# A new order of attention's instruction queues, and eight units in place of four in a turn of its loop

## The chip, the cores and the metric

One core of one Trainium2 chip runs the whole program. The time is that of one execution on the device in microseconds (us); of several runs of one kernel the median counts. The engines are TensorE (PE, with its weight loads as PEld), VectorE (DVE), ScalarE (ACT), GpSimd (POOL) and SyncE (SP, which here only issues DMAs). Each works through its own list of instructions strictly in order, and they meet only at semaphores.

## What is computed

A decoder layer on x of 4 x 512 x 512 in float32: attention of the delta-rule kind with two decay rates, then a state-space mixer with a second input, then a feed-forward block with eight low-rank experts; after each, a layer norm over the sum with the residual. The part that the change touches is attention:

```python
def step(S, inp):                                  # for each head and batch, over 512 tokens
    qt, kt, vt, bt, gt = inp
    Sd = S * gt[..., None]
    v_pred = jnp.einsum('bhk,bhkv->bhv', kt, Sd)
    S_new = Sd + jnp.einsum('bhk,bhv->bhkv', kt * bt[..., None], vt - v_pred)
    ot = jnp.einsum('bhk,bhkv->bhv', qt, S_new)
    return (S_new, ot)
...
q = short_conv(x @ wq, conv_q_w).reshape(B, T, H, DK)      # k and v likewise, H = 16, DK = DV = 128
# beta, decay and lam come from a small MLP on |v|, |v - k @ proxy_w|, their cosine and an entropy
o_fast = delta_rule(qs, k_unit, v, beta_fast, decay_fast)
o_slow = delta_rule(qs, k_unit, v, beta_slow, decay_slow)
o = lam[..., None] * o_fast + (1.0 - lam[..., None]) * o_slow
g = (x @ g1_w @ g2_w + g2_b).reshape(B, T, H, DV)
o = o / rms * onorm_w * jax.nn.sigmoid(g)
return o.reshape(B, T, H * DV) @ wo
```

## The kernel before

`attn_stage` handles 64 units, one for each head and batch, batches innermost. The 512 tokens of a unit are four chunks of 128. Each unit passes through a pipeline that is six units deep, so that in one slot the engines work on several units at once: the projections and convolutions of the unit three (K, V) or two (Q) ahead, its norms and the small MLP, the decay products and the inverse of the triangular matrices of the unit itself, the recurrence over the four chunks of the unit before it, and the output gate and the store of older ones.

There is no scheduler. In each engine's block a function `slot(s)` writes out by hand the order of that engine's steps, `s` being the unit; `late = s.at(-1)` names the same step for the slot before, which lets a step that belongs to unit n stand at the start of the next slot. `over_units` calls the slot for units -3 to 5 in straight code, then for four units in each turn of a hardware loop (13 turns, 52 units), then for the rest in straight code. In the loop the values that a wait looks for are worked out from the turn (`due`, `head_due`, `head`).

The steps that the prediction speaks of, by the functions they are in:

- PE: `products(level)`, seven levels (L525 for levels 0 to 4, L531 for 5, L535 for 6); each multiplies slices of `ks` and `nq`. `w_fine_sum` (L549) and `x_fine_sum` (L560), steps of the inverse. `recur_even` (L573 turns `ks`, L578 multiplies `nq` with the state), `recur_u` (L593), `recur_odd` (L605, L609, L616): the recurrence. `project` (L503): one of four steps of a 128x512 projection of K, V or Q. Small steps: `turn_feats` (L713), `hidden_1` (L718), `hidden_2` (L722), `heads_out` (L726), `turn_v` (L666), `proxy_v` (L672), `gate_logits` (L706), `turn_rows` (L697), `mean_square` (L692); `w_64_sum` (L650) and `y_64_sum` (L658).
- DVE: `decay_nq(level)` (L1175 twice, then L1183), which waits for `products(level)` and which `products(level + 1)` waits for; `seed_y` (L1221), `keep` (L1194), `turn_x0` (L1227), `grow` (L1203, L1207); `convolve` (L1151, three instructions); `new_state` (L1234, L1238), `residual` (L1254); `prepare_nq` (L1306, L1310), once for -k and once for the query, after which `products(0)` of the next unit may run; `set_diag` (L1214), which waits until POOL's `spread_apt` (L1459) has read `apt_fine` of the unit before.
- ACT: copies from PSUM, `tap` (L846), `silu` (L858), `exp_e1` (L1018), `exp_tot` (L1023), `root_rows` (L1029), `log_mean` (L995), `log_err` (L991), `hide_1` (L906), `copy_feats` (L1038), `copy_w` (L867, L870, L873). When a function is of another table set than the last, an ACT_TABLE_LOAD stands ahead of it.
- SP: the rows that carry gates and decays go to DRAM and come back broadcast to all partitions, four waits and loads one after another.

## Time and profile before

| | us |
|---|---|
| median of 3 runs | 4910.75 |
| lowest and highest | 4907.41, 4925.25 |
| profiled execution | 4893.68 |
| its span, first to last instruction | 4891.9 |
| attention, first to last `mean_square` | 264 to 3326 of the span |
| PE busy in the span | 4244.3 (87%) |
| DVE, ACT, POOL busy in the span | 3329.3, 2248.5, 834.9 |

The rest of the span is the state-space mixer (to about 4119) and the feed-forward block, which the change leaves alone. "Idle before" at a group or a row is how long its engine did nothing before it, with who ended that; "issue" means that it waited for no event that the profile shows. L692 runs once for each unit, so the starts of its rows mark the units. PEclk is the granted clock as a share of the full 2.4 GHz; 0.5 is 1.2 GHz.

### The profile page before, as it was taken

The page shows a single profiled execution, that of the slowest core. Times are in us where ns is not written, and L with a number is a line of the kernel's source. Part 1 is how long each engine was busy: PE and PEld are TensorE (multiplying, and loading weights), DVE is VectorE, ACT ScalarE, POOL GpSimd, SP SyncE. Part 2 cuts the span into 40 slices and gives each one's busy share as a digit, 9 for nine tenths or more (in the row PEclk, how much of TensorE's full clock was granted, in tenths as well). Part 3 has the DMA queues.
Part 4 walks back from the last instruction along what each step waited for, and adds up shares of the span by engine and source line. Part 5 has one row for each costly group of instructions (what it writes and reads, how often), then busy time and mean ns, then how long its engine had stood idle before and what let it go on. Part 6 is the DMA issues. An engine that isn't in the chain of part 4 may idle for free. (4 is left out here: it accounts for less than half of the span.)

```text
span 4891.9 us, 184831 instructions
## 1 busy us (share of the span) xinstructions
PE 4244.3 (87%) x76786; PEld 2657.1 (54%) x76786; DVE 3329.3 (68%) x5635; ACT 2248.5 (46%) x5484; POOL 834.9 (17%) x1800
## 2 busy tenths in 40 slices
PE   6789898988989888898988899975887786999999
PEld 4566666665666656666666666662333333444444
DVE  2678787777778777787777777864999995122121
ACT  2455565655556555555555555644344432111111
POOL 0222222322222222222222232220000000000000
PEclk9899999999999999999999999987898997999999
DMA  1111211112121111211111111112232334000000
GB/s 50 61 52 57 62 49 54 62 45 68 43 65 52 52 60 43 66 52 53 58 53 59 58 53 56 62 45 104 78 95 82 91 95 160 1 26 9 18 18 9
DMA packets 131630, 278.08 MB, mean 57 GB/s; under 512 B 20668, under 2 KB 62032, under 8 KB 127200
## 3 DMA queue, kind: packets, MB, share of 16 engines
q1 hardware_dynamic: 126176, 258.29, 16.8%
q8 instruction: 641, 10.50, 0.9%
q10 hardware_dynamic: 4608, 7.60, 0.4%
q14 instruction: 205, 1.68, 0.1%
HBM read 235.17 MB, written 30.67 MB: 54 GB/s over the span
## 5 line engine op out<-in xcount | busy, mean ns | idle before, releaser
L503 PE MATMUL a_pb<-a_x_t,a_w_qkv 128*128 128x512 f32 x1536 | 825.0, 634 | 24.4 <-DMA a_w_qkv<-in_w_qkv 12.2
L1175 DVE TENSOR_TENSOR a_nq<-a_nq,a_tot 128x512 f32<-128x512 f32 x768 | 516.8, 714 | 157.4 <-PE a_pb L535 62.1
L1151 DVE SCALAR_TENSOR_TENSOR a_acc<-a_pb,a_taps,a_acc 128x511 f32<-128x511 f32 (+2 forms) x576 | 429.7, 746 | 67.0 <-ACT a_acc L846 35.3
L1773 PE MATMUL m_p_y<-m_h,m_ident 128*128 128x512 f32 x512 | 292.2, 686 | 143.3 <-DVE m_h L1973 143.3
L525 PE MATMUL a_pb<-a_nq,a_ks 128*32 128x32 f32 x20480 | 250.6, 201 | 145.1 <-DVE a_ks L1183 126.6
L503 PEld LDWEIGHTS a_pb<-a_x_t,a_w_qkv 128*128 128x128 f32 x1536 | 250.4, 195 | 131.2 <-issue 104.6
L525 PEld LDWEIGHTS a_pb<-a_nq,a_ks 128*32 128x32 f32 x20480 | 218.6, 112 | 188.4 <-DVE a_nq L1175 135.2
L2241 PE MATMUL f_pb<-f_x_t,f_w_gu 128*128 128x512 f32 x704 | 308.0, 592 | 0.0
L549 PE MATMUL a_pb<-a_x_fine,a_apt_fine 32*32 32x16 f32 x16384 | 203.7, 183 | 107.3 <-issue 106.0
L1967 DVE TENSOR_TENSOR_SCAN m_h<-m_da,m_h 128x2048 f32<-128x2048 f32 x64 | 283.1, 4424 | 5.9
L549 PEld LDWEIGHTS a_pb<-a_x_fine,a_apt_fine 32*32 32x32 f32 x16384 | 173.5, 108 | 203.5 <-issue 189.8
L560 PEld LDWEIGHTS a_pb<-a_w_fine,a_y_fine 32*32 32x32 f32 x16384 | 176.9, 109 | 189.5 <-issue 178.9
L1183 DVE TENSOR_TENSOR a_ks<-a_ks,a_tot 128x512 f32<-128x512 f32 x384 | 274.5, 715 | 0.0
L2295 ACT ACTIVATE f_gate<-f_pb 128x512 f32<-128x512 f32 x132 | 78.8, 597 | 411.7 <-PE f_pb L2241 275.4
L1773 PEld LDWEIGHTS m_p_y<-m_h,m_ident 128*128 128x128 f32 x512 | 107.5, 220 | 293.4 <-DVE m_h L1973 170.2
L560 PE MATMUL a_pb<-a_w_fine,a_y_fine 32*32 32x16 f32 x16384 | 207.7, 183 | 66.1 <-issue 61.4
L1737 PE MATMUL m_p_o<-m_w_o,m_o_t 128*128 128x512 f32 x512 | 256.9, 622 | 0.0
L1194 DVE COPY_PREDICATED a_apt_fine<-a_mask_u,a_pb 128x256 f32<-128x256 int32 x320 | 179.4, 561 | 106.5 <-PE a_pb L549 106.4
L1896 ACT ACTIVATE m_da<-m_delta,m_neg_a 128x511 f32<-128x511 f32 x256 | 166.7, 711 | 182.5 <-DVE m_h L1967 180.1
L885 ACT COPY a_u_sb<-a_pb 128x256 f32<-128x256 f32 x256 | 95.4, 373 | 296.0 <-PE a_pb L593 296.0
L2241 PEld LDWEIGHTS f_pb<-f_x_t,f_w_gu 128*128 128x128 f32 x704 | 133.4, 190 | 166.4 <-issue 166.4
L2373 DVE TENSOR_TENSOR f_h_base<-f_gate,f_pb 128x512 f32<-128x512 f32 x44 | 30.2, 686 | 277.6 <-ACT f_gate L2295 277.6
(278 smaller groups left out, 8927.3 us busy)
## 6 DMA issues: line engine op xcount, KB each, us to landing
a_rows<-rows SPq DMA_DIRECT2D x192, 512.0 KB, 3.9
a_amp_sums<-amp_sums SPq DMA_DIRECT2D x64, 508.0 KB, 3.6
attn_o<-a_o_t SPq DMA_DIRECT2D x64, 256.0 KB, 2.6
m_b_rows<-ssm_bc SPq DMA_DIRECT2D x64, 256.0 KB, 3.7
m_c_rows<-ssm_bc SPq DMA_DIRECT2D x64, 256.0 KB, 4.6
m_o_t<-attn_o SPq DMA_DIRECT2D x14, 1024.0 KB, 8.6
a_w_qkv<-in_w_qkv SPq DMA_DIRECT2D x51, 256.0 KB, 2.8
f_w_gu<-in_w_gu SPq DMA_DIRECT2D x3, 1536.0 KB, 17.3
```

The lines of the kernel that those rows point to most:

```text
L503: mm = nc.tensor.matmul(pb[:, V_BANK if i == P_V else KQ_BANK], w_qkv[:, i, k], x_t[:, k, b * T:(b + 1) * T], start=(k == 0), stop=(k == D ...
L525: mm = nc.tensor.matmul(out.rearrange("p k (s h) -> p k s h", h=hs), ks[:, n2, rate, at], right(nq[:, n2, rate, :, at], hs), start=True, s ...
L549: mm = nc.tensor.matmul(w_psum[q, i].rearrange("p (s h) -> p s h", h=hs), apt_fine[q, i, NEG_K], left(x_fine[q, i:i + 1], hs)[:, 0], start ...
L560: mm = nc.tensor.matmul(x_psum[q, i], y_fine[q, i], w_fine[q, i], start=True, stop=True, tile_position=(g * BW, g * BW))
L1151: last = nc.vector.scalar_tensor_tensor(acc[:, i, d:T], src[:, 0:T - d], taps[:, i, 3 - d:4 - d], acc[:, i, d:T], ALU.mult, ALU.add)
L1175: last = nc.vector.tensor_tensor(part, part, spread(blocks, shape), ALU.mult)
L1183: nc.vector.tensor_tensor(part, part, spread(blocks.rearrange("p (s two) -> p s two", two=2)[:, :, 1:2], [P, T // hs, hs]), ALU.mult).then ...
L1194: nc.vector.copy_predicated(right(apt_fine[:].rearrange("p i k t -> p (i k) t"), hs), spread(compact(mask_u[:, level:level + 1], hs), [P, ...
L1737: mm = nc.tensor.matmul(p_o[:], o_t[:, q % 2, head], w_o[:, head], start=(head == 0), stop=(head == H - 1), skip_group_check=True)
L1773: nc.tensor.matmul(p_y[:, et], ident[:], h[:, (b * DS + n) % 3, et], start=(n == 0), stop=(n == DS - 1), skip_group_check=True).then_inc(s ...
L1967: nc.vector.tensor_tensor_scan(steps, da[:, row % 2].rearrange("p e t -> p (e t)"), steps, 0.0, ALU.mult, ALU.add).then_inc(scanned, 1)
L2241: mm = nc.tensor.matmul(out, w_gu[:, side, k, cols], x2_t[:, b % 2, k], start=(k == 0), stop=(k == DC - 1), skip_group_check=True)
```

## The change

Three things. The loop's turn has eight units (`PER_TURN = 2 * B`), so 52 units are six turns, and four more units stand in straight code behind it; `due`, `head_due`, `head` and `stored_due` follow. The steps of PE, ACT, DVE and POOL stand in another order. And the waits are fitted to that order: `keep(1)` waits for `products(1)`, the column `decay` is loaded ahead of `exp_tot`, which now comes first, and POOL drains at the start of two steps.

```diff
-FIRST_TURN, TURNS = 6, (UNITS - 12) // B
+FIRST_TURN, PER_TURN = 6, 2 * B
+TURNS = (UNITS - 12) // PER_TURN
...
     with engine.Fori(0, TURNS) as turn:
-        for j in range(B):
+        for j in range(PER_TURN):
             slot(Slot(FIRST_TURN + j, turn))
-    for n in range(FIRST_TURN + B * TURNS, UNITS + 4):
+    for n in range(FIRST_TURN + PER_TURN * TURNS, UNITS + 4):
         slot(Slot(n))
...
                 def exp_e1(s):
-                    if s.batch(1) == 0:
-                        head_col(decay, s, 1, C_DECAY)
...
                 def exp_tot(s):
+                    if s.batch(1) == 0:
+                        head_col(decay, s, 1, C_DECAY)
...
                     if level == 0:
                         need(dve, w_sum, s.due(-1, 6, 4))
-                    elif level > 1:
+                    elif level == 1:
+                        dve.wait_ge(product, s.due(0, LEVELS, 2))
+                    else:
                         dve.wait_ge(w_sum, s.due(0, 6, level - 1))
...
                 def gates_vals(s):
+                    pool.drain()
...
                 def norms_dens(s):
+                    pool.drain()
...
                 def slot(s):
-                    soon = s.at(1)
-                    if s.has(2):
-                        make_feats(s)
-                    if s.has(0):
-                        spread_y(s)
...
+                    late = s.at(-1)
+                    if late.has(1):
+                        gates_vals(late)
+                    if late.has(0):
+                        spread_apt(late)
+                    if late.has(2):
+                        norms_dens(late)
```

On PE, from `products(0)` to `products(1)`, both on the same line: before,

```order
L525 MATMUL a_pb<-a_nq,a_ks 32x32 x32
L569 REGISTER_ALU
L573 MATMUL a_pb<-a_sum_w,a_ks 128x128 x2
L503 MATMUL a_pb<-a_x_t,a_w_qkv 128x512
L593 MATMUL a_pb<-a_r_sb,a_y_inv 128x128 x2
L722 MATMUL a_pb<-a_hid,a_w_diag 128x128
L514 REGISTER_ALU
L525 MATMUL a_pb<-a_nq,a_ks 32x32 x32
```

and after:

```order
L526 MATMUL a_pb<-a_nq,a_ks 32x32 x32
L651 MATMUL a_pb<-a_x_half,a_apt 64x64 x8
L504 MATMUL a_pb<-a_x_t,a_w_qkv 128x512
L570 REGISTER_ALU
L574 MATMUL a_pb<-a_sum_w,a_ks 128x128 x2
L714 MATMUL a_pb<-a_sum_w,a_feats 16x128
L656 REGISTER_ALU
L659 MATMUL a_pb<-a_y_inv,a_w 64x64 x8
L515 REGISTER_ALU
L526 MATMUL a_pb<-a_nq,a_ks 32x32 x32
```

`w_64_sum`, `turn_feats` and `y_64_sum` have come in between; `recur_u(0)` and `hidden_2` now stand between `products(1)` and `products(2)`, with `hidden_1`, `w_fine_sum(1)` and `recur_odd(0)`.

On DVE, from `decay_nq(0)` to what follows `decay_nq(1)`: before,

```order
L1175 TENSOR_TENSOR a_nq<-a_nq,a_e 128x512 x2
L1183 TENSOR_TENSOR a_ks<-a_ks,a_e 128x512
L1221 COPY_PREDICATED a_y_fine<-a_mask_u,a_pb 128x128
L123 REGISTER_ALU
L1194 COPY_PREDICATED a_apt_fine<-a_mask_u,a_pb 128x256
L1227 STREAM_TRANSPOSE a_x_fine<-a_y_fine 128x256
L1163 REGISTER_ALU
L1175 TENSOR_TENSOR a_nq<-a_nq,a_tot 128x256x2 x2
L1183 TENSOR_TENSOR a_ks<-a_ks,a_tot 128x256x2
L1231 REGISTER_ALU
L1234 COPY a_state<-a_pb 128x256
```

and after:

```order
L1230 STREAM_TRANSPOSE a_x_fine<-a_y_fine 128x256
L1193 REGISTER_ALU
L1197 COPY_PREDICATED a_apt_fine<-a_mask_u,a_pb 128x128x2
L1176 TENSOR_TENSOR a_nq<-a_nq,a_tot 128x256x2 x2
L1184 TENSOR_TENSOR a_ks<-a_ks,a_tot 128x256x2
L1149 REGISTER_ALU
L1152 SCALAR_TENSOR_TENSOR a_acc<-a_pb,a_taps,a_acc 128x511
L1152 SCALAR_TENSOR_TENSOR a_acc<-a_pb,a_taps,a_acc 128x510
L1152 SCALAR_TENSOR_TENSOR a_acc<-a_pb,a_taps,a_acc 128x509
L1234 REGISTER_ALU
L1237 COPY a_state<-a_pb 128x256
```

`keep(1)` has moved ahead of `decay_nq(1)`, and `convolve` of Q ahead of `new_state(0)`. Before `decay_nq(0)` stand now, in this order, `set_diag`, `convolve` of K, `prepare_nq` of -k, `grow(4)`, `decay_nq(6)`, `prepare_nq` of the query, `invert` and `convolve` of V.

On ACT, from `root_rows` on to the end of a slot: before,

```order
L1029 ACTIVATE a_rroot_rows<-a_logs_o 128x512
L861 REGISTER_ALU
L873 COPY a_w<-a_pb 64x512
L1021 ISA
L1023 ACTIVATE a_tot<-a_amp_sums,a_decay 128x1016
L906 ACT_TABLE_LOAD
L906 ACTIVATE a_hid<-a_pb,a_bias 128x128
L917 COPY a_o_t<-a_pb 128x128
L858 ACTIVATE a_kq<-a_acc 128x512
L1033 COPY a_y_inv<-a_pb 64x8x64
```

and after, from the copies of `copy_xy32` on:

```order
L1002 COPY a_x_half<-a_pb 32x8x32
L1006 COPY a_y_inv<-a_pb 32x8x32 x2
L992 ACT_TABLE_LOAD
L992 ACTIVATE a_feats<-a_norms 128x4
L862 REGISTER_ALU
L874 COPY a_w<-a_pb 64x512
L859 ACT_TABLE_LOAD
L859 ACTIVATE a_kq<-a_acc 128x512
L1039 COPY a_feats_t<-a_pb 16x128
L1034 COPY a_y_inv<-a_pb 64x8x64
L918 COPY a_o_t<-a_pb 128x128
```

`log_err` has moved from behind `log_mean` to behind the exponentials, so a unit now has four table loads on ACT (L996, L1024, L992, L859) where it had three (L995, L1018, L906).

## Rows read from the trace of the kernel before

**Rows 1.** The page: busy time of each engine, share of the span, instructions.
```profile
PE 4244.3 (87%) x76786; PEld 2657.1 (54%) x76786; DVE 3329.3 (68%) x5635; ACT 2248.5 (46%) x5484; POOL 834.9 (17%) x1800
```

**Rows 2.** Timeline of PE, `mean_square`: start, length, engine, line, operation, idle before.
```profile
264.25 1.02 PE L692 MATMUL a_pb<-a_o_sq,a_mean_w 128*128 128x512 f32 x2
...
554.56 1.02 PE L692 MATMUL a_pb<-a_o_sq,a_mean_w 128*128 128x512 f32 x2
...
611.63 1.20 PE L692 MATMUL a_pb<-a_o_sq,a_mean_w 128*128 128x512 f32 x2
...
2961.87 1.02 PE L692 MATMUL a_pb<-a_o_sq,a_mean_w 128*128 128x512 f32 x2
...
3202.60 1.07 PE L692 MATMUL a_pb<-a_o_sq,a_mean_w 128*128 128x512 f32 x2
```

**Rows 3.** Windows: straight code and loop; stretch, length, busy time of each engine, PEclk, DMA.
```profile
264.00:555.00 291.00, 261.63 (x6894) 184.98 (x6893) 230.51 (x459) 169.88 (x457) 78.13 (x169) 0.98 0.17 55
555.00:2962.00 2407.00, 2129.33 (x55105) 1512.31 (x55104) 1854.56 (x3684) 1353.05 (x3636) 624.30 (x1345) 0.96 0.18 55
```

**Rows 4.** Waits from 555 to 2962 (48 units): us in total, times, longest.
```profile
PE a_pb L525 <- DVE a_ks L1183: 98.0, 132, 1.3
PE a_pb L549 <- issue: 83.5, 47, 3.8
PE a_pb L560 <- issue: 42.9, 41, 2.3
```

**Rows 5.** Timeline of PE where one turn of the loop ends.
```profile
1194.02 0.61 PE L697 MATMUL a_pb<-a_sum_w,a_vals 128*24 128x255 f32 x2
1198.01 0.72 PE L549 MATMUL a_pb<-a_x_fine,a_apt_fine 32*32 32x16 f32 x64 [3.38 <-issue]
...
1199.32 1.06 PE L609 MATMUL a_pb<-a_nq,a_state 128*128 128x128 f32 x4
```

**Rows 6.** Timeline of PE around `products` 0 to 3 of a unit inside a turn.
```profile
1280.65 1.14 PE L658 MATMUL a_pb<-a_y_inv,a_w 64*64 64x64 f32 x16
1281.72 0.76 PE L525 MATMUL a_pb<-a_nq,a_ks 128*32 128x32 f32 x64
...
1284.57 0.75 PE L525 MATMUL a_pb<-a_nq,a_ks 128*32 128x32 f32 x64 [0.19 <-DVE a_ks L1183]
...
1288.11 0.75 PE L525 MATMUL a_pb<-a_nq,a_ks 128*32 128x32 f32 x64 [0.96 <-DVE a_ks L1183]
...
1293.91 0.75 PE L525 MATMUL a_pb<-a_nq,a_ks 128*32 128x32 f32 x64 [0.88 <-DVE a_ks L1183]
...
1296.63 0.73 PE L549 MATMUL a_pb<-a_x_fine,a_apt_fine 32*32 32x16 f32 x64
...
1297.84 0.61 PE L609 MATMUL a_pb<-a_nq,a_state 128*128 128x128 f32 x4
```

**Rows 7.** Timeline of DVE from `convolve` of V to `decay_nq(1)` of the next unit.
```profile
1275.78 2.39 DVE L1151 SCALAR_TENSOR_TENSOR a_acc<-a_pb,a_taps,a_acc 128x511 f32<-128x511 f32 x3 [0.25 <-ACT a_acc L846]
1278.49 1.22 DVE L1306 TENSOR_TENSOR a_nq<-a_kq,a_rows 128x1024 f32<-128x1024 f32 x1 [0.32 <-PE a_pb L609]
1279.79 1.23 DVE L1310 TENSOR_TENSOR a_nq<-a_nq,a_e 128x1024 f32<-128x1024 f32 x1
...
1282.52 1.30 DVE L1175 TENSOR_TENSOR a_nq<-a_nq,a_e 128x512 f32<-128x512 f32 x2 [1.15 <-PE a_pb L525]
1283.73 0.68 DVE L1183 TENSOR_TENSOR a_ks<-a_ks,a_e 128x512 f32<-128x512 f32 x1
...
1286.07 1.30 DVE L1175 TENSOR_TENSOR a_nq<-a_nq,a_tot 128x512 f32<-128x512 f32 x2 [0.16 <-issue]
```

**Rows 8.** Timeline of ACT: a table load and what it is for.
```profile
1279.90 1.28 ACT L906 ACT_TABLE_LOAD   x1
1281.19 0.37 ACT L906 ACTIVATE a_hid<-a_pb,a_bias 128x128 f32<-128x128 f32 x1
```

**Rows 9.** Timeline of POOL: `spread_apt`.
```profile
1274.60 2.74 POOL L1459 COPY a_apt<-a_apt_fine 32x256 f32<-32x256 f32 x4
```

More of the change, by code:

```diff
@@ L731, in slot @@
                     if late.has(0):
+                        x_fine_sum(late, 1)
+                    if late.has(2):
+                        proxy_v(late)
+                    if late.has(-3):
+                        gate_logits(late)
+                    if late.has(0):
+                        products(late, 3)
+                    if late.has(-1):
+                        recur_u(late, 1)
+                    if late.has(1):
+                        turn_rows(late)
+                    if late.has(0):
                         w_fine_sum(late, 2)
@@ L734, in slot @@
                         recur_odd(late, 1)
+                    if late.has(-2):
+                        mean_square(late)
                     if late.has(0):
                         products(late, 4)
-                    if late.has(0):
-                        x_fine_sum(late, 2)
+                    if late.has(3):
+                        project(late, 3, P_K, 0)
                     if late.has(-1):
@@ L742, in slot @@
                         project(late, 3, P_K, 1)
-                    if late.has(2):
-                        gram_kq(late)
                     if late.has(0):
-                        w_fine_sum(late, 3)
+                        x_fine_sum(late, 2)
+                    if late.has(-1):
+                        recur_u(late, 2)
                     if late.has(0):
@@ L749, in slot @@
                     if late.has(-1):
-                        recur_u(late, 2)
-                    if late.has(-2):
-                        mean_square(late)
+                        recur_odd(late, 2)
+                    if late.has(0):
+                        w_fine_sum(late, 3)
+                    if late.has(2):
+                        gram_kq(late)
+                    if late.has(3):
+                        project(late, 3, P_K, 2)
+                    if late.has(-1):
+                        recur_even(late, 3)
+                    if late.has(3):
+                        project(late, 3, P_K, 3)
                     if late.has(0):
@@ L784, in slot @@
                         project(s, 2, P_Q, 0)
-                    if late.has(-1):
-                        recur_u(late, 3)
+                    if late.has(0):
+                        xy_32_sum(late)
+                    if s.has(2):
+                        project(s, 2, P_Q, 1)
+                    if s.has(0):
+                        products(s, 0)
                     if late.has(0):
                         w_64_sum(late)
-                    if late.has(-1):
-                        recur_odd(late, 3)
-                    if s.has(2):
-                        project(s, 2, P_Q, 1)
-                    if s.has(1):
-                        hidden_1(s)
                     if s.has(2):
                         project(s, 2, P_Q, 2)
+                    if s.has(-1):
+                        recur_even(s, 0)
+                    if late.has(2):
+                        turn_feats(late)
                     if late.has(0):
@@ L1316, in slot @@
                     if late.has(0):
-                        decay_nq(late, 0)
-                    if late.has(0):
                         seed_y(late)
-                    if late.has(0):
-                        keep(late, 0)
                     if late.has(0):
@@ L1353, in slot @@
                         decay_nq(late, 4)
+                    if late.has(-1):
+                        residual(late, 2)
+                    if late.has(-3):
+                        gate_o(late)
                     if late.has(0):
                         grow(late, 2)
+                    if late.has(0):
+                        decay_nq(late, 5)
                     if late.has(-1):
-                        residual(late, 2)
+                        new_state(late, 2)
+                    if late.has(0):
+                        keep(late, 4)
+                    if late.has(-1):
+                        residual(late, 3)
                     if late.has(2):
```

220 lines of the change are left out of this document (95 added, 125 removed).

## The prediction

> **What bounds the kernel now.** The page first [rows 1]: PE is busy for 87% of the span, DVE for 68%, ACT for less than half. The change touches attention alone, so the question is what one unit costs there and what PE does in it. The starts of `mean_square` [rows 2] give the unit. In straight code, 264.25 to 554.56, six units take 290.3 us, 48.4 each; at the end, 2961.87 to 3202.60, again in straight code, five take 240.7, 48.1 each. In the loop between them, 554.56 to 2961.87, 48 units take 2407.3, 50.15 each or 200.6 for a turn of four. The same four units in straight code would be 193.5. So a turn costs 7.1 us more than its work, and the units do not share it: the one across the first loop end, 554.56 to 611.63, takes 57.1.
>
> The windows [rows 3] say the same from the side of PE: it is busy for 261.6 of 291 us (43.6 a unit) in straight code and for 2129.3 of 2407 (44.4 a unit) in the loop, and its clock falls from 0.98 to 0.96. PE is nearly the bound: the unit is 44 us of its work and 4 to 6 of idle time. The waits [rows 4] name this idle time. 98.0 us in 48 units, 2.04 a unit, are `products` waiting for `decay_nq` on DVE; the others are "issue", where PE waited for no event that shows.
>
> **Part 1, eight units in a turn.** At a loop end PE finishes `turn_rows` at 1194.63 and starts the next step at 1198.01, 3.38 us later [rows 5]; inside a turn no such gap stands there, the same step at 1296.63 follows with no idle time before it [rows 6]. After the gap PE runs at the lower of its two clocks, 1.2 GHz: the four matmuls of L609 take 1.06 us there [rows 5] against 0.61 inside a turn [rows 6]. Gap, clock and what the other engines lose at their own loop ends make up the 7.1. The old loop has 13 turns, so 12 jumps back; the new one 6 turns, so 5. Seven jumps fewer at 7.1 is **50 us**. Bounds: below, the gap alone, 7 x 3.4 = 24; above, 7 x 8.0 = 56 if the tail's 48.1 is the right straight unit. I take 50, since the whole-turn difference counts everything. Nothing covers a jump on PE, and the jump in the new order also stands where PE has work waiting (`recur_even(1)` to `x_fine_sum(1)`), so I price one jump as before.
>
> The Trainium skill, Runtime: NRT & Kernel Launch, section Instruction fetch mechanics, says that a taken branch to a target outside the window forces a fetch of the target page, and that otherwise fetch hides behind issue. The trace agrees with the first half, 3.38 us at the jump. It speaks against the second: L560 and L549 lose time to "issue" in the middle of runs of small matmuls as well.
>
> **Part 2, the new order: what it removes.** In the unit of rows 6 the three waits of `products` 1, 2 and 3 are 0.19, 0.96 and 0.88, together 2.03, as the mean of 2.04 says [rows 4]. Each is DVE being late by what stands between two decays.
> - `products(1)`: `decay_nq(0)` runs from 1282.52 to 1284.41 [rows 7], 1.9 us, and PE has only 1.9 us of other work after `products(0)`. The new order puts `w_64_sum`, one step of `project`, half of `recur_even`, `turn_feats` and `y_64_sum` there. `y_64_sum` takes 1.07 from start to start [rows 6], `w_64_sum` is of the same size, with the others some 3.7 us: covered by 1.6.
> - `products(2)`: DVE starts `decay_nq(1)` 1.66 us after the end of `decay_nq(0)` [rows 7]. PE now has `project`, `hidden_1`, `recur_u(0)`, `w_fine_sum(1)`, `hidden_2` and `recur_odd(0)` before it, about 3.8 us; DVE needs about 3.9 from the end of `decay_nq(0)` and PE arrives at 4.7. Covered.
> - `products(3)`: `convolve` of Q (2.39, rows 7) still stands in front of `decay_nq(2)`, but PE arrives at about 9.5 against DVE's 9.0. Just covered.
>
> **Part 2: what it adds.** `convolve` of Q now stands ahead of `new_state(0)`, and `recur_even(1)` waits for that. DVE reaches the state at 3.9 + 2.4 + 0.4 = 6.7 us after the end of `decay_nq(0)`, PE arrives at 6.0: about 0.8 of wait that was not there. `products(0)` waits for `prepare_nq` of the query; between K's last `project` and it DVE has `convolve` of K (2.39), -k (2.5), `grow(4)`, `decay_nq(6)` (2.0) and the query (1278.49 to 1281.02, 2.5) [rows 7], about 10.4 from a start some 2.2 later, against 12.4 us of PE steps: 0 to 0.4 of wait. What PE loses to "issue" delays PE and not DVE, so part of these waits is hidden by it. The sum added is 0 to 1.5, and I take 1.0; net the order is worth 2.0 - 1.0 = 1.0 us a unit. Over about 58 full units that is **58 us**, with bounds of 0.5 (29) and 2.0 (118). All else that moved on PE keeps PE's work as it is.
>
> ACT gets a fourth table load each unit, 1.28 us [rows 8]. It stands between `copy_xy32` and `copy_w(6)`, which releases `y_64_sum`. Meanwhile PE has the rest of `w_64_sum`, a `project` and `recur_even(0)`, and by my walk ACT has 0.8 us to spare; ACT is busy for 28 of 49 us [rows 3]. I cost it at nothing; without the cover it would be 1.28 a unit, 74 us in all. The added drains on POOL are cheap, since it is busy for a quarter of the unit [rows 3]. SP's chain of loads starts from the same `turn_rows` and keeps its place.
>
> The Trainium skill, ScalarE: Activation LUTs, section What ACT_TABLE_LOAD costs, gives a switch 1283 ns and a drain of about 1380 more, 2.66 us in all. Here the function starts at 1281.19, 1.29 us after the load started at 1279.90 [rows 8]: the load agrees, the drain does not show. By the page's 2.66 the 0.8 to spare would be short by 0.6 us a unit, 35 us in all, and the time some 4838.
>
> **The sum.** 50 + 58 = 108 us off the profiled execution's 4893.7: 4785.7. The median of the runs lies 17.1 above that execution, so **4803 us**.
>
> **The rivals.**
> - Only the loop pays (chance 0.20). The order trades waits one for one: the 2.0 removed come back at `recur_even(1)` and `products(0)`. For it: DVE is busy for 38.6 of 50 us a unit [rows 3] and the new waits all hang on its long steps. Against it: the steps that I can place have room. 4911 - 50 = 4861, give or take 20.
> - The order hides everything (0.19). "issue" on PE covers the added waits, and with fewer gaps the clock stays up: the loop's mean of 0.96 against 0.98 [rows 3] is 1 us a unit. 2.0 + 0.3 a unit over 58 is 133, with the loop 183: about 4735 to 4780, say 4765.
> - Slower (0.08): `set_diag` blocks DVE. It has moved from the end of DVE's slot to ahead of `convolve` of K, and waits for `spread_apt`, 2.74 us [rows 9], which starts only after `keep(4)` and which POOL now does behind `gates_vals`. My walk has it 0.6 us early. If POOL is late, each us goes through `convolve` of K, `prepare_nq` and `products(0)` straight to PE. The gains end once DVE is held for more than 2.0 + 0.9 (the loop's 50 over 58) - 0.3, so from about 2.6 us a unit; at 3.2 the time is some 4945.
> - The fourth table load is not covered (0.05). The 0.8 us that ACT has to spare is the thinnest of the margins; with none of it, `y_64_sum` and with it `products(1)` are late by up to 1.28 us [rows 8], which is at most 74 us in all, 4877, and half of it, 4840, is the likelier size, since DVE makes PE wait near there anyway. The drain that the page on ScalarE adds would be such a case.
> - The jump costs more than before, or the loop's gain doesn't come since other engines lose more at theirs: inside the first rival's range.
>
> **How the numbers follow.** Forecast 4803 with 0.48, within 4780 to 4835. What a measurement of this kernel can tell from no change is about 0.5%, 25 us, that is 4886 to 4935. Faster by more than that holds the forecast, the second rival, most of the first and the fourth: 0.48 + 0.19 + 0.13 + 0.04 = 0.84; within it 0.09, the first rival's upper end and mild forms of the third; slower 0.07. The range, 4755 to 4880, leaves out the third and the tips of the others.
>
> **What would show it.** In the profile after: five gaps of about 3.4 us on PE between `recur_even(1)` and `x_fine_sum(1)` at a distance of some 390 us, and none else of this size; straight units of 47 to 47.5 us by `mean_square` and a turn of eight of about 7 more than eight of these; the wait of L526 for `a_ks` down from 98 us to under 30 over 48 units; a new wait of `recur_even` (L579) for `a_state`, up to 0.8 a unit; four table loads a unit on ACT and no wait of PE for ACT at `y_64_sum` or `hidden_1`. The forecast is wrong if the straight unit stays at 48.4 (then only the loop paid), if "issue" on PE grows past 4 us a unit, or if DVE idles ahead of `set_diag`.

## The result, and the profile after

The median went from 4909.1 us (four runs, 4906.2 to 4925.3) to **4587.6 us** (four runs, 4584.9 to 4595.4): ratio 0.9341, 95% interval 0.9317 to 0.9365, 322 us less where 106 were forecast. Lines of the kernel after are one to five further down than before: `products` is L526, `w_fine_sum` L550, `x_fine_sum` L561, `mean_square` L693.

The page of the kernel after, against [rows 1]: as many matmuls, 76786, in 60.1 us less busy time.

```profile
PE 4184.2 (91%) x76786; PEld 2616.5 (57%) x76786; DVE 3306.2 (72%) x5635; ACT 2299.2 (50%) x5544; POOL 963.4 (21%) x1800
```

Windows of the kernel after (stretch, length, busy time of PE, PEld, DVE, ACT, POOL with counts, PEclk, DMA share, GB/s), six straight units and the 48 units of the loop, against [rows 3]:

```profile
242.00:507.00 265.00, 257.50 (x6890) 182.95 (x6888) 228.37 (x460) 174.34 (x462) 88.70 (x168) 1.00 0.19 60
507.00:2668.00 2161.00, 2076.22 (x55105) 1476.03 (x55104) 1836.17 (x3685) 1394.42 (x3685) 726.99 (x1344) 0.99 0.20 61
```

A straight unit is 44.2 us (48.4 before), a loop unit 45.0 (50.15). The loop stretch has 55105 matmuls in both kernels, so the two can be set side by side. It is 246 us shorter: PE's busy time falls by 53.1 (2129.3 to 2076.2) for the same matmuls; its idle time falls by 193, from 277.7 to 84.8. The busy time fell with the clock: by the clock records of the two traces PE worked 185 us of it at 1.2 GHz before and 37 after, and at most half of that difference, 74 us, could come back. What the idle time was, the waits of PE in that stretch say (us in total, times, longest), against [rows 4]:

```profile
PE a_pb L561 <- issue: 17.9, 14, 4.0
PE a_pb L526 <- DVE a_nq L1313: 12.5, 26, 0.8
PE a_pb L606 <- ACT a_u_sb L886: 9.9, 5, 2.2
PE a_pb L651 <- POOL a_y_inv L1479: 9.6, 42, 0.4
PE a_pb L550 <- issue: 8.0, 18, 1.0
...
PE a_pb L574 <- DVE a_state L1237: 5.2, 22, 0.3
...
PE a_pb L526 <- DVE a_ks L1184: 3.2, 17, 0.2
```

The wait for the decays is gone (98.0 to 3.2) and what replaces it is small. But the largest fall is in "issue": the two groups of [rows 4] alone were 126.4, all lines together 173.5; now all are 38.0. So the 246 us are 135.5 of issue, 55.4 of waits for other engines (98.0 to 42.6), 53.1 of clock, and a rest of 2. Not all of this "issue" is of one kind: the idle time at the loop ends, between `turn_rows` and `w_fine_sum` before and between `recur_even(1)` and `x_fine_sum(1)` after, is under the same name. It is 39.9 us of the 173.5 and 13.9 of the 38.0, so 26 of the 135.5 belong to the loop.

PE's timeline in a unit of the loop shows why the waits went. `products` 0 to 2, 850.86 to 861, in the order that [rows 6] had otherwise:

```profile
850.86 0.76 PE L526 MATMUL a_pb<-a_nq,a_ks 128*32 128x32 f32 x64 [0.47 <-DVE a_nq L1313]
851.84 1.11 PE L651 MATMUL a_pb<-a_x_half,a_apt 64*64 64x64 f32 x16 [0.22 <-POOL a_y_inv L1479]
...
854.48 1.14 PE L659 MATMUL a_pb<-a_y_inv,a_w 64*64 64x64 f32 x16
855.55 0.76 PE L526 MATMUL a_pb<-a_nq,a_ks 128*32 128x32 f32 x64
...
860.41 0.76 PE L526 MATMUL a_pb<-a_nq,a_ks 128*32 128x32 f32 x64
...
862.08 0.44 PE L574 MATMUL a_pb<-a_sum_w,a_ks 128*128 128x128 f32 x2
```

DVE's timeline at the same time: the decays end at 855.31 and 859.39, 0.2 and 1.0 us before PE comes for them, and `new_state(0)` at 862.02, just before PE's 862.08.

```profile
854.62 0.69 DVE L1184 TENSOR_TENSOR a_ks<-a_ks,a_e 128x512 f32<-128x512 f32 x1
...
858.70 0.69 DVE L1184 TENSOR_TENSOR a_ks<-a_ks,a_tot 128x512 f32<-128x512 f32 x1
859.30 2.39 DVE L1152 SCALAR_TENSOR_TENSOR a_acc<-a_pb,a_taps,a_acc 128x511 f32<-128x511 f32 x3
861.61 0.41 DVE L1237 COPY a_state<-a_pb 128x256 f32<-128x256 f32 x1
```

And a loop end, to be read against [rows 5]: the gap is the same, and so is the lower clock behind it (`gate_logits`, L707, takes 1.91 us here and 1.02 inside a turn). The unit around it, 683.71 to 738.19, takes 54.5 us.

```profile
683.71 1.02 PE L693 MATMUL a_pb<-a_o_sq,a_mean_w 128*128 128x512 f32 x2
...
720.17 1.22 PE L606 MATMUL a_pb<-a_apt,a_u_sb 128*128 128x128 f32 x4 [1.67 <-ACT a_u_sb L886]
...
724.95 0.61 PE L579 MATMUL a_pb<-a_state,a_nq 128*128 128x128 f32 x4
729.00 1.05 PE L561 MATMUL a_pb<-a_w_fine,a_y_fine 32*32 32x16 f32 x64 [3.44 <-issue]
729.98 2.08 PE L673 MATMUL a_pb<-a_proxy,a_kq 128*128 128x128 f32 x8
731.85 1.91 PE L707 MATMUL a_pb<-a_g_t,a_g 128*128 128x512 f32 x2
```

### The profile page after: what moved, and what is told of

Same layout as the page of the kernel before. It is cut to its first block and busy times, and to the rows that moved or that the text cites. A ratio compares the mean times of both kernels' runs of the same rounds, so it can differ in the third digit from the quotient of the medians.

```text
span 4588.4 us, 184268 instructions
## 1 busy us (share of the span) xinstructions
PE 4184.2 (91%) x76786; PEld 2616.5 (57%) x76786; DVE 3306.2 (72%) x5635; ACT 2299.2 (50%) x5544; POOL 963.4 (21%) x1800
## 5 line engine op out<-in xcount | busy, mean ns | idle before, releaser
L504 PE MATMUL a_pb<-a_x_t,a_w_qkv 128*128 128x512 f32 x1536 | 838.2, 638 | 12.6 <-DMA a_w_qkv<-in_w_qkv 12.1
L526 PEld LDWEIGHTS a_pb<-a_nq,a_ks 128*32 128x32 f32 x20480 | 215.5, 112 | 213.1 <-issue 117.9
L526 PE MATMUL a_pb<-a_nq,a_ks 128*32 128x32 f32 x20480 | 253.0, 201 | 49.2 <-DVE a_nq L1313 31.8
L1464 POOL COPY a_apt<-a_apt_fine 32x256 f32<-32x256 f32 x256 | 100.8, 394 | 936.9 <-DVE a_apt_fine L1197 912.1
L504 PEld LDWEIGHTS a_pb<-a_x_t,a_w_qkv 128*128 128x128 f32 x1536 | 239.7, 191 | 96.0 <-issue 59.7
L561 PEld LDWEIGHTS a_pb<-a_w_fine,a_y_fine 32*32 32x32 f32 x16384 | 165.5, 106 | 175.2 <-issue 166.8
L847 ACT ACTIVATE a_acc<-a_pb,a_taps 128x512 f32<-128x512 f32 x192 | 132.0, 688 | 214.4 <-PE a_pb L504 214.4
L1479 POOL COPY a_y_inv<-a_y_fine 32x256 f32<-32x256 f32 x256 | 223.0, 871 | 32.8
L561 PE MATMUL a_pb<-a_w_fine,a_y_fine 32*32 32x16 f32 x16384 | 192.9, 181 | 23.8 <-issue 23.0
```

Of the source, the lines that this page charges most:

```text
L504: mm = nc.tensor.matmul(pb[:, V_BANK if i == P_V else KQ_BANK], w_qkv[:, i, k], x_t[:, k, b * T:(b + 1) * T], start=(k == 0), stop=(k == D ...
L526: mm = nc.tensor.matmul(out.rearrange("p k (s h) -> p k s h", h=hs), ks[:, n2, rate, at], right(nq[:, n2, rate, :, at], hs), start=True, s ...
L561: mm = nc.tensor.matmul(x_psum[q, i], y_fine[q, i], w_fine[q, i], start=True, stop=True, tile_position=(g * BW, g * BW))
L1479: last = nc.gpsimd.tensor_copy(y_inv[q, s.ring(0, 2), :, q], y_fine[q])
```

## The experiments

The question was why the change brought three times the sum. Differences to the kernel before are by the ratio, which compares runs of one batch, and stand with its interval. The kernel before itself came to medians from 4899.9 to 4928.3 in these batches, so differences to the kernel after are also taken from the two ratios, times 4909; where plain medians are compared, the text says so. The table takes the same 48 units, some 55105 matmuls, from each trace: the length of the stretch, PE's busy time, its idle time by "issue" and by waits for other engines (sums of the waits view), and, in us a unit over 40 of them, the part of the idle time that falls inside a run of matmuls of one line without a wait for an engine. "Issue" holds the gaps at the loop ends too; the column after the waits doesn't. The last column is worked out from the records of the trace: PE's working time, idle time taken out, per 16 KB of its instructions (254 records of matmuls and weight loads), over stretches of five such blocks; of all these stretches it gives the fifth percentile, that is the densest ones.

| kernel | median | 48 units | PE busy | issue | waits | inside runs, a unit | us a block |
|---|---|---|---|---|---|---|---|
| before | 4909 | 2407 | 2129 | 173.5 | 98.0 | 2.5 | 3.52 |
| e1, old order, 8 units | 4870 | 2369 | 2114 | 161 | 89 | 2.7 | 3.46 |
| e12, old order, no loop | 4809 | 2336 | 2097 | 152 | 85 | 2.9 | 3.44 |
| e3, K spread | 4910 | 2417 | 2150 | 162 | 98 | 2.1 | 3.66 |
| e6, small loads | 4884 | 2369 | 2114 | 147 | 102 | 2.0 | 3.48 |
| e11, jump moved | 4878 | 2398 | 2122 | 179 | 91 | 2.5 | 3.51 |
| after | 4588 | 2161 | 2076 | 38 | 43 | 0.5 | 4.28 |
| e2, new order, 4 units | 4638 | 2213 | 2106 | 50 | 51 | 0.3 | 4.30 |
| e5, new order, no loop | 4544 | 2112 | 2056 | 29 | 25 | 0.5 | 4.25 |
| e4, K clustered | 4640 | 2202 | 2077 | 35 | 86 | 0.4 | 4.08 |
| e8, more loads | 4628 | 2190 | 2088 | 57 | 41 | 0.8 | 4.31 |
| e10, K in one block | 4694 | 2233 | 2093 | 47 | 89 | 0.8 | 3.86 |
| e9, products(0) later | 4706 | 2249 | 2097 | 31 | 118 | 0.4 | 4.21 |
| e7, products(0) last | 4895 | 2389 | 2201 | 19 | 167 | 0.2 | 4.25 |

**The two parts alone.** The old order with eight units in a turn:

```diff
-FIRST_TURN, TURNS = 6, (UNITS - 12) // B
+FIRST_TURN, PER_TURN = 6, 2 * B
+TURNS = (UNITS - 12) // PER_TURN
```

> The old order of the queues, with eight units in a turn: the loop's part of the change alone. Theory A (the order of PE's queue did most, because it spreads the runs of small matmuls so that instruction blocks last longer than their fetch): seven jumps fewer at 7 us, so about 4858 (4850 to 4870); a straight unit stays at 48.4 us and PE's idle time inside runs of small matmuls stays at some 2.4 us a unit. Rival B (the longer turn changed how code is fetched, and with it the stalls in every unit): well under 4800, with straight units near 46.

Measured: 4870.0, ratio 0.9942 (0.9923 to 0.9961), 28 us less, at the upper end of theory A; the stalls inside runs stayed at 2.7 us a unit. And the new order with four units in a turn:

```diff
-FIRST_TURN, PER_TURN = 6, 2 * B
+FIRST_TURN, PER_TURN = 6, B
 TURNS = (UNITS - 12) // PER_TURN
```

> The new order of the queues, with four units in a turn: the order's part alone. Theory A: 12 jumps at about 8 us and units of 44.2 us, so 4588 + 7 x 8 = 4644 (4630 to 4660). Rival B: about 4800, since the stalls come back with the short turn.

Measured: 4637.6, ratio 0.9447 (0.9411 to 0.9482), 271 us less. The order is nearly all of it. With the same twelve jumps on both sides (before against e2) the 48 units are 194 us shorter: 123 of issue, 47 of waits, 24 of clock. From here to the kernel after the loop gives 50 us by medians (52 by the ratios and in the 48 units), seven jumps at 7.1, as forecast; in the old order the same seven gave 28 by the ratio, 4.0 each, and 38 in the 48 units, 5.4 each. No run reordered the queue of one engine alone, so which part of the new order removed the stalls was not separated.

**No loop at all**, in both orders:

```diff
-    for n in range(-3, FIRST_TURN):
-        slot(Slot(n))
-    with engine.Fori(0, TURNS) as turn:
...
-    for n in range(FIRST_TURN + PER_TURN * TURNS, UNITS + 4):
+    for n in range(-3, UNITS + 4):
```

> The changed kernel without a loop: all 68 slots in straight code, no jump at all. The loops so far put a jump at 7.1 us in the new order (4637.6 with 12 jumps, 4587.6 with 5). If a jump costs what it does there: 5 x 7.1 = 36 us less, 4552 (4540 to 4562). Rival: straight code costs something that a loop doesn't (longer register or wait code, fetch from more memory): above 4565.

> The old order with no loop at all: the straight code of all units, the counterpart of the new order's straight run. Theory: what the two orders differ by is not in the loop. A jump of the old order was worth 28 to 30 us for seven of them, 4.2 each, so the other five of the eight-unit loop give 5 x 4.2 = 21: 4870 - 21 = 4849 (4835 to 4865), and the idle time inside runs of one line stays at 2.3 to 3.0 us a unit, the dependency waits at 2.0 to 2.5, the clock loss at .7 to 1.9. The new order's gain without any loop is then 4849 - 4544 = 305. Rival: a good part of the stalls and of the clock loss is brought about by the loop (the buffers of instructions start anew at each jump); then straight code of the old order runs near 4780 to 4820, with stalls under 2 us a unit.

Measured: new order 4544.3, ratio 0.9214 (0.9177 to 0.9251), inside the range expected; **it beats both kernels**. Old order 4809.3, ratio 0.9797 (0.9772 to 0.9822): 100 us less than before, 40 more than the theory had, in the range of the rival, but without its mechanism, since the stalls inside runs stayed at 2.9 us a unit. So the loop costs about 100 us in the old order (100 by the ratio) and 93 to 114 in the new (by medians and by ratios). What the two windows say of 48 units, old order and then new:

```profile
552.00:2888.00 2336.00, 2097.10 (x55103) 1485.97 (x55103) 1853.74 (x3685) 1353.96 (x3636) 611.49 (x1344) 0.97 0.18 57
```
```profile
509.00:2621.00 2112.00, 2055.51 (x55109) 1462.94 (x55109) 1834.94 (x3687) 1397.10 (x3686) 718.59 (x1344) 1.00 0.21 63
```

This is the cleanest view of the order, with no jump in it: 224 us in 48 units, of which issue 123 (55%), waits for engines 60 (27%), clock 42 (19%). The largest waits of the old one (this kernel's lines stand five ahead of before's: L520 is `products`, L544 and L555 the two fine sums):

```profile
PE a_pb L520 <- DVE a_ks L1178: 85.0, 125, 1.4
PE a_pb L544 <- issue: 54.3, 44, 2.9
PE a_pb L555 <- issue: 43.7, 47, 2.2
```

**What "issue" is.** Away from the loop ends such a stall stands in the middle of work that waits for nobody. PE's timeline of the kernel before shows both kinds: 2.83 us at a loop end, between `turn_rows` and `w_fine_sum`, and 2.15 us between two matmuls of one step of `project`. Each is followed by matmuls at 1.2 GHz (L609 1.06 us against 0.61 in [rows 6], L503 1.22 for one matmul):

```profile
597.22 0.72 PE L549 MATMUL a_pb<-a_x_fine,a_apt_fine 32*32 32x16 f32 x64 [2.83 <-issue]
...
598.49 1.06 PE L609 MATMUL a_pb<-a_nq,a_state 128*128 128x128 f32 x4
...
602.87 0.59 PE L503 MATMUL a_pb<-a_x_t,a_w_qkv 128*128 128x512 f32 x1
605.61 1.22 PE L503 MATMUL a_pb<-a_x_t,a_w_qkv 128*128 128x512 f32 x1 [2.15 <-issue]
```

The clock goes with the same stalls. In the 48 units of the kernel before, the granted clock falls 43 times; the longest idle time near the fall is an "issue" stall 42 times, loop ends among them, and a wait for the decays once. Without a loop in the old order (e12) it is 32 falls, 31 of them near such a stall. In the kernel after there are 9 falls, in e5 none.

In the records of the trace, stalls inside runs end 1.2 to 1.5 us after a packet of the instruction queue has ended; such packets take 0.9 to 1.5 us, mostly, and in a stretch of 2000 us of the kernel before nineteen in twenty of them started at least 3.6 us after the one before. That made PE's instruction supply the suspect, by three theories in turn.

The first: dense runs of small matmuls next to each other use a block up too fast, so breaking them up with `project` (few, long matmuls) in the old order should help, and clustering in the new one should hurt.

```diff
                         products(late, 4)
+                    if late.has(3):
+                        project(late, 3, P_K, 1)
...
                         w_fine_sum(late, 3)
+                    if late.has(3):
+                        project(late, 3, P_K, 2)
```

> The kernel before with two statements of PE's queue moved and nothing else: a step of K's projection (1 us of PE in 4 instructions' worth of code) from behind recur_even(2) to between products(4) and x_fine_sum(2), and another from behind x_fine_sum(3) to between w_fine_sum(3) and products(5). Each long matmul now stands inside a run of small ones. Theory A (blocks of instructions are used up faster than the next is fetched): the stalls inside runs fall from 2.4 to about 1.5 us a unit and the clock dips with them, 50 to 90 us less in all, about 4830. Rival C (the stalls come from the broadcast loads that share the DMA engines with the fetch, wherever the small matmuls stand): no change beyond 10 us, 4900.

Measured: 4910.4, ratio 1.0022 (1.0002 to 1.0043), no gain where 50 to 90 us were expected. The stalls inside runs fell from 2.5 to 2.1 only, and PE's busy time rose by 21 us, so what they gave was lost again in the clock. The converse, K0 and K1 taken from behind `products(4)` and `recur_even(2)` to stand directly ahead of K2:

```diff
-                    if late.has(3):
-                        project(late, 3, P_K, 0)
...
-                    if late.has(3):
-                        project(late, 3, P_K, 1)
...
+                    if late.has(3):
+                        project(late, 3, P_K, 0)
+                    if late.has(3):
+                        project(late, 3, P_K, 1)
                     if late.has(3):
                         project(late, 3, P_K, 2)
```

> The changed kernel with two statements of PE's queue moved: the first two steps of K's projection from among products(4), recur_even(2) and w/x_fine_sum(2) to behind gram_kq, next to the third. The run of small matmuls from w_fine_sum(2) to gram_kq then has nothing long in it. Theory A: stalls inside runs rise from 0.5 to 1.5 to 2.5 us a unit, PE's clock falls below 0.98, and the time rises by 60 to 120 us, to about 4670. Rival C (place among the loads, not density): within 15 us of 4588. Rival D (it was the waits for DVE that went, and the stalls only followed): the wait of products for DVE rises, since PE reaches products(4) and (5) up to 1.9 us earlier; then the added time is in L526 and L532 with DVE named.

Measured: 4640.1, ratio 0.9451 (0.9421 to 0.9482), 54 more than after (41 in the 48 units), but not through stalls: issue stayed at 35, and a new wait is all of it, `recur_u(2)` for DVE's residual:

```profile
PE a_pb L594 <- DVE a_r_sb L1257: 47.0, 46, 1.1
```

Both expectations failed. Local density is not it.

The second theory: PE's instruction fetches are slowed by the broadcast loads that share the DMA engines. In the old order, the loads of `rows` and `amp_sums` cut to an eighth (the rest of these tiles stays zero, so this kernel's output is not the layer's):

```diff
-                            sp.dma_start(rows[:, q:q + 2].rearrange("p q t -> p (q t)"),
...
+                            sp.dma_start(rows[:, q, 0:P],
...
-                        sp.dma_start(amp_sums[:], spread(io["amp_sums"][r].unsqueeze(0), [P, PAIRS * SUMS])
+                        sp.dma_start(amp_sums[:, 0:SUMS], spread(io["amp_sums"][r][0:SUMS].unsqueeze(0), [P, SUMS])
```

> The kernel before, in which the three broadcast loads of rows and the one of sums read and write an eighth of their size (64 KB in place of 512 KB, and the rest of the tiles stays at zero, so decays and rows are not those of the reference; queues, waits and instruction counts are the same). Rival C (the broadcasts that share the DMA engines make the instruction fetch late): the stalls inside runs fall from 2.47 us a unit to under 0.8, the clock loss with them, and the time to about 4750. Theory A2 (over stretches of three to five blocks the old order uses up a block in 3.1 to 3.5 us, while one fetch follows another in no less than 3.6 even when nothing else runs): the stalls stay above 1.5 us a unit, time 4840 to 4890.

Measured: 4883.6, ratio 0.9902 (0.9871 to 0.9933). The window of 48 units shows the DMA share down from 0.18 [rows 3] to 0.07, and issue only from 173.5 to 147:

```profile
557.00:2926.00 2369.00, 2114.17 (x55106) 1503.25 (x55107) 1854.71 (x3685) 1353.62 (x3636) 622.18 (x1345) 0.97 0.07 19
```

The packets of the instruction queue were as long as before, 1.16 us in the mean against 1.15. And the other way, four further loads of 512 KB a unit in the new order:

```diff
+                        for again in range(4):
+                            sp.dma_start(extra[:], spread(io["rows"][r, 0:2 * TT].rearrange("q t -> (q t)").unsqueeze(0),
+                                                          [P, 2 * T])).then_inc(extra_in, 16)
+                            hold(extra_in, s.due(1, 64, 16 * (again + 1)))
```

> The changed kernel with four more broadcast loads of 512 KB for each unit, one after another, into a tile that nobody reads, issued by SP behind the load of the query's rows. No engine waits for them; only the DMA engines are busier, about 16 us more in each unit of 44. Theory A2 (the fetch has a margin of some 0.2 us a block left in the new order, 3.9 us against 3.6 to 3.7): a fetch that takes 1.5 us longer during these loads has no margin, so the stalls inside runs rise from 0.5 to 1.5 to 3 us a unit and the time by 80 to 200 us. If the fetch doesn't bound anything here: within 15 us of 4588.

Measured: 4627.8, ratio 0.9391 (0.9356 to 0.9426), 25 more than after by the ratios and 29 in the 48 units (40 by medians of different batches), well under the 80 to 200 expected; the DMA share was 0.34 against 0.20, issue 57 against 38. So other traffic moves the stalls by 19 to 26 us in 48 units, and is not what tells 173.5 from 38.

The third theory is the rate over longer stretches, the last column of the table. The old order has stretches of five blocks in which PE works a block off in 3.4 to 3.7 us, about the distance in which the fetches follow each other; in the new order these take 4.3. Between the two orders the stalls inside runs go with it: 2.0 to 2.9 us a unit at 3.44 to 3.66, 0.2 to 0.8 at 3.86 to 4.31. Inside the old order they hardly do: 2.0 at 3.48 (e6), 2.7 at 3.46 (e1). It was drawn up after e3 to e8 were seen, so it needed a run of its own: in the new order all four steps of K behind `x_fine_sum(3)` (the places that they leave are not shown).

```diff
+                    if late.has(3):
+                        project(late, 3, P_K, 0)
+                    if late.has(3):
+                        project(late, 3, P_K, 1)
+                    if late.has(3):
+                        project(late, 3, P_K, 2)
+                    if late.has(3):
+                        project(late, 3, P_K, 3)
```

> The new kernel, with the four steps of the projection of K put behind x_fine_sum(3) in one block rather than spread over the places ahead of it. The theory of the rate of instruction blocks: a stretch of TensorE's program that uses up a 16 KB block in less than the 3.6 us in which the instruction fetches follow each other runs dry, whatever the engines' waits are. This puts a dense run of small matmuls (w_fine, x_fine with nothing between) at 3.3 to 3.5 us a block, and it expects the idle time inside runs of one line to rise from .48 to at least 1.5 us a unit, and 4587.6 + 58 x 1.0 to 2.0 = 4646 to 4704. Rival: such idle time in the old kernel came from its own layout as a whole; then it stays under .8 us a unit. Either way the steps of K no longer cover what VectorE and ScalarE hand back there, so waits of TensorE for them may come in place of it: if these are over 1 us a unit and the idle inside runs stays under .8, the theory is not borne out by this run (the wait has given the fetch its time), and the time is then 4640 to 4700 by the waits alone.

Measured: 4693.9, ratio 0.9563 (0.9527 to 0.9599), 109 more than after. The stalls inside runs rose, from 0.48 to 0.83 us a unit, but to half of the 1.5 expected; the densest stretches came to 3.86 and not to 3.5 over five blocks, and the wait of e4 came back beside them:

```profile
PE a_pb L594 <- DVE a_r_sb L1257: 46.6, 47, 1.1
PE a_pb L561 <- issue: 22.3, 26, 2.2
```

The direction is as the theory has it, the size is not. Nor does the direction decide: e8 has the same 0.8 us a unit with its densest stretches unchanged at 4.31. By its own terms the run misses the 1.5 that the theory asked for and stands just above the 0.8 under which the theory was to be given up. So the rate of instructions goes with the stalls between the two orders, but no run shows that it causes them. The cause of the stalls stays open.

**What a wait costs.** In the new order `products(0)` was moved from behind `recur_odd(1)` to stand right ahead of `products(1)`, so that nothing covers `decay_nq(0)`:

```diff
-                    if s.has(0):
-                        products(s, 0)
...
+                    if s.has(0):
+                        products(s, 0)
                     if s.has(0):
                         products(s, 1)
```

> The changed kernel with one statement of PE's queue moved: products(0) from behind project(P_Q, 1) to behind y_64_sum, right ahead of products(1), so nothing covers decay_nq(0) any more. If the cover is what removed the wait there, PE waits 2.1 us a unit for a_ks at products(1) (a decay of 1.9 and two hand-overs), less the 0.27 that products(0) waits now and less what that wait gives the fetch: about +1.7 us a unit, 110 us in all, 4700 (4670 to 4720). Rival D (the waits only take up time that PE loses elsewhere anyway): under 4640.

Measured: 4895.2, ratio 0.9937 (0.9919 to 0.9955), where 4700 was expected: one step moved takes back 293 of the 324 us (both by the ratios; 308 of 322 by medians). The wait itself was as forecast, 2.09 us a unit, and another came with it:

```profile
PE a_pb L526 <- DVE a_ks L1184: 100.1, 48, 2.1
PE a_pb L651 <- POOL a_y_inv L1479: 55.4, 47, 1.8
```

But the waits explain 124 us of the 228 in 48 units; as much again, 125, is PE's busy time, 2201 against 2076 for the same matmuls, while issue fell by 19. Timeline of PE at one of these waits, and the window behind it:

```profile
673.97 0.77 PE L526 MATMUL a_pb<-a_nq,a_ks 128*32 128x32 f32 x64
676.82 0.92 PE L526 MATMUL a_pb<-a_nq,a_ks 128*32 128x32 f32 x64 [2.09 <-DVE a_ks L1184]
677.67 2.08 PE L504 MATMUL a_pb<-a_x_t,a_w_qkv 128*128 128x512 f32 x2
...
687.32 0.46 PE L574 MATMUL a_pb<-a_sum_w,a_ks 128*128 128x128 f32 x2
687.62 0.61 PE L579 MATMUL a_pb<-a_state,a_nq 128*128 128x128 f32 x4
```
```profile
677.20:687.40 10.20, 10.20 (x197) 7.86 (x188) 6.55 (x13) 3.63 (x10) 0.00 (x0) 0.50 0.01 3
```

After 2.09 us without work PE ran for 10.2 us at a granted clock of 0.50, which is 1.2 GHz, with no idle time at all. From `products(1)` to `recur_even(1)`, the same steps in the same order, it took 10.5 us here (676.82 to 687.32) and 6.5 in the unit of the kernel after shown above (855.55 to 862.08): 4.0 us lost on top of a wait of 2.1. That happened in some units and not in others. Of the 47 falls of the granted clock in this stretch, 35 have the wait of 2.1 us as the longest idle time near them and 9 the wait for POOL; PE did 368 us of its work at 1.2 GHz, and the mean granted clock was 0.92. And `products(0)` put behind `turn_feats`, with `y_64_sum` alone left between it and `products(1)`:

```diff
-                    if s.has(0):
-                        products(s, 0)
...
+                    if s.has(0):
+                        products(s, 0)
```

> The new kernel, with products(0) moved from behind recur_odd(1) to behind turn_feats(late), that is two groups of matmuls ahead of products(1) rather than right ahead of it as in the run in which it stood last, or far ahead as in the new kernel. The cover of the wait for VectorE's a_ks is then y_64 alone, some 1.07 us of TensorE's work. Dependency theory: products(1) waits 2.1 - 1.07, about 1.0 us a unit, and y_64's neighbours on GpSimd's a_y_inv another 0.5 to 1.2 us, where the new kernel waits 0.1 and 0.2. If a wait of about 1 us costs no more than itself: 1.3 to 2.0 us a unit over 58 units, 4587.6 + 75 to 116 = 4663 to 4704, and the clock lost stays at about 0.5 us a unit. Rival: the clock answers to a wait of 1 us as it did to one of 2.1 us (3.8 us a unit lost on top): 4587.6 + 58 x (1.3 + 3.8) = 4883 or so. What tells them apart is the granted clock over the loop: .98 to .99 by the first, about .91 by the rival.

Measured: 4706.5, ratio 0.9589 (0.9561 to 0.9617), 122 more than after, at the upper end of the first theory; the waits were 0.9 and 1.2 us a unit, the granted clock 0.98. In 48 units 76 us more of waits brought 20 of busy time through the clock: 1.3 us for each us waited, or 1.2 with the 7 us of issue that went. In e4, 43 us of waits of 1.0 each brought 1 of busy time. In e7 124 us of waits brought 125: 2.0 for one, or 1.8 with the 19 of issue that went. So waits of about 1 us cost themselves or a little more, and e7's cost nearly twice themselves. No run has the wait of 2.1 us alone: e7 and e9 share the wait of 1.2 us for POOL, so what is shown is the step from 0.9 to 2.1 beside it.

**Where the jump stands.** Since a jump was worth less in the old order, the loop of the kernel before was entered two units later:

```diff
-FIRST_TURN, TURNS = 6, (UNITS - 12) // B
+FIRST_TURN, TURNS = 8, (UNITS - 12) // B
```

> The kernel before with the loop entered two units later (first turn at unit 8 in place of 6), so that the jump back no longer falls at the place in the cycle of four units at which it fell before. In the run of the old order with eight units in a turn, one unit in four is 51 to 52 us long rather than 48.7 even without a jump, and a jump there cost only some 4 us beyond that, while it cost 7 to 8 in the new order. Theory: in the old kernel jump and long unit fall together and partly hide each other. Apart, twelve jumps lose that shelter, 12 x about 3 us: 4909 + 36 = 4945 (4930 to 4960), with units of 54 to 55 us and of 51 to 52 us side by side. Rival: the jump costs the same anywhere, and the smaller gain of eight units in the old order has another cause: 4905 to 4915.

Measured: 4878.4, ratio 0.9944 (0.992 to 0.9967): 27 less by the ratio, where 36 more were expected (the two traced executions differ by 12). The theory falls. In the loop nothing changed: from the ninth `mean_square` to the 57th it is 2398.9 us before and 2397.7 here; one unit of four took 54.6 and the one ahead of it 51.3, but with their neighbours at 45.7 and 48.2 the turn was as long as before. What differs in the traces lies outside this stretch. Why seven jumps are worth 50 us in one order and 28 (38 in the 48 units) in the other was not settled.

## Why the prediction was wrong

**The bound** was read rightly: PE sets the unit, and its idle time is what can be won.

**Part 1, the loop, 50 us.** Right in the new order (e2 to after, 50.0) and in what was said of the place: gaps between `recur_even(1)` and `x_fine_sum(1)` at 725.6, 1450.0 and 1812.0 of 3.4 to 4.0 us. They come every 362 us and not every 390, since the units are shorter; of the five, the one at 1088 was 2.06 us and the one at 2175.5 was 0.77. A jump also reaches PE through ACT, five waits at L606 together 9.9 us, which the sum had under "what the other engines lose". But the 7.1 us a jump were read off the old order, and there seven jumps proved worth 28 by the ratio and 38 in the 48 units, 4.0 to 5.4 each. That the new order gave just 50 is in part luck.

**Part 2, the waits.** The walk held for `products(2)` and `products(3)`, less so for `products(1)`. In sum they went from 98.0 to 3.2 us, "under 30" was said. But `products(1)` was to be covered by 1.6 us and was by 0.2: `decay_nq(0)` did not end 2.1 us after `products(0)` but 3.7 (851.62 to 855.31), since DVE still had `convolve` of V to finish. `new_state(0)` on DVE ended 6.7 us after `decay_nq(0)`, as reckoned; PE came not at 6.0 but at 6.8, since the steps ahead, up to `heads_out` and `turn_v`, took longer than the walk gave them, so the new wait of 0.8 a unit was 5.2 us in all, and it showed at L574 and not at L579. `products(0)` waited 12.5 us, 0.26 a unit, inside the 0 to 0.4. Not foreseen was `w_64_sum` waiting for POOL, 9.6 us, 0.2 a unit. In sum 1.0 us a unit was forecast as net gain; the pair without loops gives 60.4 / 48 = 1.26, before and after 55.4 / 48 = 1.15. This term was mis-sized by little.

**The fourth table load** cost nothing that shows, as said: ACT counts 60 more instructions, and PE waits for ACT at neither `y_64_sum` nor `hidden_1`. No wait for POOL stands among DVE's waits in the loop, so `set_diag` held nobody there and the rival that ended slower had no case.

**The step that failed** is the premise under which the waits were turned into time: everything else on PE stays as it is. Beside the gaps at the loop ends, which Part 1 counts, the prediction took "issue" as a fixed load that the change could only worsen ("wrong if it grows past 4 us a unit"), and put no gain on it; without the loop ends it fell from 133.6 to 24.1 us, and with them from 173.5 to 38.0. And it held the clock of Part 2 at its level, where 53 us came back in the 48 units. By the pair without loops these two are 3.4 us a unit, against 1.26 of waits: 165 of 224 us. Straight units of 47 to 47.5 were forecast and 44.2 came. Why the order removed the stalls is open; that it did, the pair without loops shows. The rival that hides everything named the clock, with 0.3 us a unit against the 0.9 measured, and let "issue" cover waits; none had it go. Its own sum, 183 off 4911, gives 4728, not the 4765 that it states.

The rows that would have shown it were there: L549 and L560 lose 126 of 278 idle us to "issue" [rows 4], and twelve jumps at the 3.4 us of [rows 5] are only 41 of it. Over all lines some 118 us (2.5 a unit) stood inside runs that wait for nobody, more than the 98.0 of the decays. The prediction noted that this spoke against fetch being hidden and drew nothing from it for the sum. The Trainium skill, Runtime: NRT & Kernel Launch, section Instruction fetch mechanics, says that instructions come in blocks of 16 KiB and that their fetch hides behind issue. The first half agrees with the instruction queue's packets, 16384 bytes each; against the second stand the 152 us of issue in code without any jump (e12), if they are waits for a fetch, which the packets that end just before them suggest and no run proves.

## What to carry to other kernels

Idle time by "issue" in the middle of runs of small matmuls is not a constant of the code: an order of the same instructions removed most of it here, and where it is larger than the waits for engines it should carry a term of its own in any sum, split into loop ends and the rest. A wait on a PE that is nearly full was worth one to two times its length here, through the clock; the longest should be removed first, and an order that has none is fragile, as one step moved here cost 293 of 324 us. Where the program may be as long as it likes, the loop itself is worth a run without it.

## What the runs showed of the hardware

- After a wait of 2.09 us PE's granted clock stood at 0.50 for 10.2 us of uninterrupted work (e7, in some units only); of the 43 falls of the granted clock in 48 units of the kernel before, 42 stood near a stall with nothing to wait for or a loop end; without a loop and with 57 us of idle time in 2112 the granted clock was 1.00 over that stretch (e5).
- PE stalled for 2.0 to 2.9 us a unit with nothing to wait for inside runs in every kernel of the old order, loop or not, and 0.2 to 0.8 in every kernel of the new one. More than halving the other DMA traffic (share 0.18 to 0.07) took away 26 of 173.5 us, and raising it from 0.20 to 0.34 added 19.
- A hardware loop over this code, 12 jumps and its entry and exit, cost about 100 us in the old order and 93 to 114 in the new, though the gaps that show on PE at its jumps are 39.9 us in all in the kernel before, 3.3 each.
